# Two reorderings in a fused convolution and feed-forward kernel: the conversion of h in tile 21, and tile 1's first silu and up product

## What is computed

```python
def fake_quant(t, axis):
    s = jnp.max(jnp.abs(t), axis=axis, keepdims=True) / QMAX
    s = jnp.maximum(s, 1e-08)
    q = jnp.clip(jnp.round(t / s), -QMAX - 1.0, QMAX) * s
    return t + jax.lax.stop_gradient(q - t)
def qlinear(x, w):
    return jnp.einsum('bsh,oh->bso', fake_quant(x, axis=-1), fake_quant(w, axis=1))
out = lax.conv_general_dilated(x, weight, window_strides=(STRIDE,), padding=[(PAD, PAD)],
                               dimension_numbers=('NCH', 'OIH', 'NCH'), feature_group_count=GROUPS)
y = out + ctx[:, :, None] + bias[None, :, None]
gate = qlinear(y, w_gate)      # 512 -> 1376
up = qlinear(y, w_up)
h = jax.nn.silu(gate) * up
x + qlinear(h, w_down)         # 1376 -> 512
```

## Time and profile before

| what | us |
|---|---|
| median of 3 runs | 294.35 |
| lowest and highest run | 294.17 and 295.05 |
| the profiled execution | 294.47 |
| its span, first to last instruction | 292.9 |

### The profile page before, as it was taken

How to read it: one execution, slowest core, us unless ns; L and a number is a source line. 1 busy time by engine, 2 the same in 40 slices (tenths; PEclk the granted TensorE clock), 3 DMA queues, 4 the chain that set the end, 5 groups by cost and what they waited for, 6 DMA issues and landing times.

```text
span 292.9 us, 4778 instructions
## 1 busy us (share of the span) xinstructions
PE 281.7 (96%) x1621; PEld 164.4 (56%) x1621; DVE 251.0 (86%) x405; ACT 194.3 (66%) x232; POOL 202.0 (69%) x213
## 2 busy tenths in 40 slices
PE   7998999999999999999999999999989999999995
PEld 7897656655455555554444556665434444444443
DVE  3879879999998988989888878897978889888885
ACT  2258999996686666564888845455688866666640
POOL 1595899998776766663788835556578887666623
PEclk9999999999999999999999999999999999999999
DMA  7999963579846877755489996524256684433355
GB/s 261 416 408 357 410 133 72 113 166 273 214 144 160 203 168 165 208 149 119 128 214 299 239 241 195 166 49 124 73 157 157 159 177 114 87 86 85 100 99 202
DMA packets 83847, 53.36 MB, mean 182 GB/s; under 512 B 69904, under 2 KB 70672, under 8 KB 83696
## 3 DMA queue, kind: packets, MB, share of 16 engines
q1 hardware_dynamic: 83536, 52.89, 67.3%
q10 hardware_dynamic: 288, 0.18, 0.3%
HBM read 27.75 MB, written 8.39 MB: 123 GB/s over the span
## 4 chain that ended last, share of the span: by engine, by line
PE 64%; DVE 9%; POOL 9%; DMA 7%; ACT 5%; issue 4%; SPq 1%; DVEq 0%; POOLq 0%
PE bank L1047 38%; PE bank L1067 19%; PE bank L931 7%; POOL sg_mem L525 4%; DMA xq_mem<-yq_mem 3%; DMA slab<-x_windows 3%; DVE h_mem L813 2%; DVE h_max L819 2%; POOL xq_mem L499 1%; DVE y_part L745 1%; DMA hq_mem<-hq_mem 1%; DVE sg_mem L803 1%; DVE gu_max L704 1%; POOL y_mem L499 1%; ACT sg_mem L635 1%
## 5 line engine op out<-in xcount | busy, mean ns | idle before, releaser
L1047 PE MATMUL bank<-wgu_t,xq_mem 128*128 128x512 bf16 (+1 forms) x768 | 155.9, 357 | 3.1 <-DVE h_mem L813 2.0
L525 POOL TENSOR_TENSOR sg_mem<-sg_mem,gu_scale_row 128x512 f32<-128x512 f32 (+1 forms) x96 | 111.4, 1163 | 64.3 <-ACT sg_mem L635 64.0
L1047 PEld LDWEIGHTS bank<-wgu_t,xq_mem 128*128 128x128 bf16 x768 | 73.7, 98 | 75.2 <-DVE h_mem L813 8.8
L635 ACT ACTIVATE sg_mem<-sg_mem,x_scale 128x512 f32<-128x512 f32 (+1 forms) x96 | 63.7, 674 | 42.5 <-DVE sg_mem L803 42.1
L1067 PE MATMUL bank<-wd_t,hq_mem 128*128 128x512 bf16 (+1 forms) x341 | 78.6, 379 | 0.5 <-DMA hq_mem<-hq_mem 0.5
L813 DVE SCALAR_TENSOR_TENSOR h_mem<-bank,x_scale,sg_mem 128x512 f32<-128x512 f32 (+1 forms) x96 | 66.2, 691 | 10.3 <-POOL sg_mem L525 9.1
L803 DVE TENSOR_TENSOR sg_mem<-bank,gu_scale_row 128x512 f32<-128x512 f32 (+1 forms) x96 | 60.3, 628 | 16.0 <-PE bank L1047 15.6
L640 ACT ACTIVATE h_mem<-h_mem,h_inv 128x1376 f32<-128x1376 f32 (+1 forms) x32 | 45.3, 1414 | 28.1 <-DVE h_inv L697 28.0
L1067 PEld LDWEIGHTS bank<-wd_t,hq_mem 128*128 128x128 bf16 (+1 forms) x341 | 33.3, 98 | 40.9 <-DMA hq_mem<-hq_mem 1.0
L819 DVE TENSOR_REDUCE h_max<-h_mem 128x1 f32<-128x1376 f32 x32 | 50.4, 1576 | 0.0
L931 PE MATMUL bank<-toeplitz_cut,slab 128*128 128x160 f32 (+1 forms) x320 | 44.6, 290 | 1.9 <-DMA slab<-x_windows 1.7
(11 more groups left out here) (63 smaller groups left out, 138.4 us busy)
## 6 DMA issues: line engine op xcount, KB each, us to landing
slab<-x_windows SPq DMA_DIRECT2D x32, 320.0 KB, 5.4
xo_mem<-x SPq DMA_DIRECT2D x24, 256.0 KB, 3.0
out<-xo_mem SPq DMA_DIRECT2D x24, 256.0 KB, 2.2
hq_mem<-w_gate_up SPq DMA_DIRECT2D x6, 512.0 KB, 6.8
slab<-w_down SPq DMA_DIRECT2D x3, 688.0 KB, 12.5
h_mem<-w_gate_up SPq DMA_DIRECT2D x4, 512.0 KB, 13.6
slab<-x SPq DMA_DIRECT2D x1, 2048.0 KB, 9.3
out<-slab SPq DMA_DIRECT2D x7, 256.0 KB, 2.0
```

Source lines behind the costliest of these rows:

```text
L525: pool.tensor_tensor(s, s, gu_scale_row[:, 1, at:at + n], ALU.mult).then_inc(silu_scaled, 1)
L635: act.activation(s, s, ACT.Silu, scale=x_scale[:, i:i + 1]).then_inc(silu_done, 1)
L1047: last = pe.matmul(bank[n % 2][:, 0:cols], xq_t[:, g, k, P * c:P * (c + 1)], wgu_t[:, m, k, at:at + cols], start=(k == 0), stop=(k == KT - 1))
```

## The change

On ACT, in tile 21, `convert_h(20)` is issued ahead of `round_y(24)` and `round_y(25)` instead of behind them. In tile 0, ACT issues `silu(1, 0)` ahead of the rounding of channels 2 and 3 instead of behind it and the copy of a span, and POOL issues `scale_silu(1, 0)` ahead of the conversion of these channels. DVE issues `multiply_up(1, 0)` ahead of `token_scales(0)`. PE and SP have the same lists as before. No instruction is added or taken away.

```diff
@@ constants @@
-        FOLDS_AT[21] = [SLOTS - 1]
+        GROUP_3_AT = 21
+        FOLDS_AT[GROUP_3_AT] = [SLOTS - 1]
@@ gpsimd @@
             for i in range(TILES):
-                scale_silu(i, 0)
+                if i != 1:
+                    scale_silu(i, 0)
@@
                 scale_silu(i, 2)
+                if i == 0:
+                    scale_silu(1, 0)
                 for n in CHANNELS_AT.get(i, []):
                     convert_y(n)
@@ scalar @@
             for i in range(TILES):
+                if i > 1:
+                    silu(i, 0)
                 if i:
-                    silu(i, 0)
                     silu(i, 1)
@@
                 if i < TILES - 1:
                     silu(i, 2)
+                if i == 0:
+                    silu(1, 0)
+                if i == GROUP_3_AT:
+                    convert_h(i - 1)
                 for n in CHANNELS_AT.get(i, []):
                     round_y(n)
@@
-                if i:
+                if i and i != GROUP_3_AT:
                     convert_h(i - 1)
@@ vector @@
+                if i == 1:
+                    multiply_up(i, 0)
                 if i:
                     token_scales(i - 1)
@@
-                multiply_up(i, 0)
+                if i != 1:
+                    multiply_up(i, 0)
```

## The result

| | time, us |
|---|---|
| before, median of 20 (quickest to slowest) | 293.77 (293.69 to 295.05) |
| after, median of 20 (quickest to slowest) | 295.19 (293.73 to 296.44) |
| ratio after / before, 95% interval | 1.0037 [1.0027, 1.0048] |
| profiled execution of after, its span | 293.81, 292.2 |
| forecast | 293.47 (292.9 to 294.2) |

What follows compares the result with a forecast made beforehand. PE was taken as the bound from 75.7 to 131 and 215 to 270 us, with PE, ACT, DVE and POOL all busy from 49.1 to 63. Terms -1.23 and +0.35 on 294.35 gave 293.47 us, range 292.9 to 294.2.

Steps and rivals of the forecast that it cites:

- Term 1: Tile 21: h's conversion fits ACT's 2.06 us hole, so tile 22's product and up(22, 2) come earlier, -1.23 us.
- its last part: The prediction's closing list of what the changed profile would show if each part of the forecast is right or wrong.
- the 213.2 that was named as the sign against this term: Tile 22: a product starting later than 213.2 would show the forecast gain of -1.23 us wrong.
- Part 2's first half: Tile 1: the early silu and scaling start the product at 42.01, so up(1, 2) no longer waits for it.
- I take a value near the lower end, 2.5: Tile 2: channel 2's transpose, issued at 42.49, lands after 2.5 us at 45.0, against 45.06 for gate(2, 0) before.
- term 2: Tiles 1 to 6: PE gains nothing in tile 1 and delay on other engines reaches it, +0.35 us (0 to +0.75).
- the two ways that led to that term: Delay reaches PE through channel 6's transpose, 0.35 us later, or through up(2, 2) waiting for a product 0.24 to 0.31 later.
- Slower, by the transpose of channel 6: Rival: shifted by 0.35 us, channel 6's transpose may need 10.0 us, PE waits 2.27 more, 295.7 us; chance 0.08.
- Absorbed: Rival: the 0.35 us delay from tile 1 is absorbed by idle time on the engines, 293.1 us; chance 0.14.
- part 2 works: Rival: in tile 1 PE keeps its 0.93 us, needing channel 2 landed by 44.0, 292.2 us; chance 0.05.

Runs made afterwards that it cites:

- Part 1 alone: The kernel before with only the conversion of h in tile 21 moved and tiles 0 and 1 untouched: median 292.98 us, ratio 0.9966.
- the change with 16 empties: The full change with 16 instead of 22 empty matmuls at PE's start: median 292.86 us, 0.9961 of before.
- the change with no move on DVE: The full change, but multiply_up(1, 0) stays behind tile 0's row maximum on DVE: median 292.84 us, 0.9964 of before.
- part 1 with 36 empties: The kernel before with only tile 21's conversion of h moved, and 36 instead of 22 empty matmuls at PE's start: median 293.74 us, 0.9968 of before.

## Why the prediction was wrong

**Term 1, -1.23 us: right.** 1.21 us measured; the conversion in the hole, no wait of POOL ahead of `scale_silu(22, 0)`, and PE's idle time before up(22, 2) gone, as its last part asks for. The product of tile 22 starts at 213.60, beyond the 213.2 that was named as the sign against this term; but everything there comes 0.67 us later through tile 2, and without that it is 212.93, against 212.92 in the working. Part 1 alone moved the median by 292.98 - 293.91 = -0.93 and the quickest by -1.2 us.

**Part 2's first half: right.** The product was forecast at 42.01 and stands at 41.93, DVE's idle time before it at 0.24 and is 0.17; `round_h(0)` was forecast at 44.66 (44.59), channel 2's issue at 42.49 (42.43). The listed wait for L813 in tile 1 is gone, and a wait for xq_mem stands one group later, as its last part asks for, though of 2.25 us and not of about 1.

**The step that failed: "I take a value near the lower end, 2.5".** The landing took 3.8 us, and PE's wait was 2.25 us, not 1. I gave 3.3 as the bad end because before had it; and I saw only the queue ahead, not what else uses the DMA engines. The ground given, that the down weights' transpose is gone by then, was nearly right (it lands 0.9 us after channel 2's issue, and behind one like it channel 2 took 2.3); what was missing is the fetch packet that falls into the transpose. With 2.3, in the change with 16 empties, PE is 0.33 us late at tile 5, against a term 2 of +0.35. Of the two ways that led to that term one came: up(2, 2) waits for the later product. The other, by channel 6, did not: there channel 6 was issued at 68.37, some 0.4 us later with the start-up taken out, but landed after 7.05 us, not 7.73, and PE no longer waited for it; that both ways had given about the same number is luck. With 3.8 the term is +1.21. The whole gain of part 1 is eaten by this: 1.21 against 1.21.

**What was missing as well: the granted clock.** No rival had it. I moved a wait of 0.93 us from one group to the next and took it to be neutral; joined with the later landing it became one idle stretch of 2.25 us, after which half of the executions lost some 1.7 to 2 us more; by their mean clock of 0.992 to 0.994 they ran some 3.5 to 4.7 us at 1.2 GHz (an estimate: 0.6 to 0.8% of 292 us, times two). It gives the change its sign: the ten executions of after that kept the clock have a median of 294.04, 0.1% above before's.

**The rivals.** "Slower, by the transpose of channel 6" had the sign and, by luck, nearly the time, 295.7, but the wrong transfer: channel 6 cost nothing, since PE's wait for it was gone; it was channel 2. "Absorbed" and "part 2 works" did not come.

A version that beats both kernels is part 1 alone: 0.9966 [0.9951, 0.9981] of before. The whole change with 16 empties (0.9961) and the change with no move on DVE (0.9964) can't be told from it.

## What to carry to other kernels

Work put ahead of the step that issues a transfer is paid for by whoever waits for that transfer: cost the landing with the long values of its line as well as the short ones, and look at which other DMA queues have a packet there, since making an engine quicker moves its instruction fetches too. Before merging two short waits of TensorE into one long one, ask what the granted clock does after it, and compare the spread of executions and their mean clock, not the profiled execution alone. A part that gains where its engine had a hole (part 1) is best timed by itself.

## What the runs showed of the hardware

- One 16 KB instruction packet took 0.9 to 1.7 us here, and a transpose of 128x512 bf16 whose packets it fell among landed after 3.8 to 4.5 us instead of 2.3 to 3.4; the down weights' after 5.4 to 5.6 instead of 3.8 to 4.7. A channel's transpose queued close behind the down weights' landed 0.5 to 0.6 us after it: after 3.3 us in before, with no such packet near, and after 4.1 in part 1 with 36 empties, where the packet had delayed the down weights.
- Of the kernel whose profiled executions have 2.25 us of PE idle time, 15 of 30 executions have a mean granted clock of 0.992 to 0.994, and of one with 2.33 us, 4 of 4; the trace of the latter shows the clock at half right behind the idle time. What decides between falling and not falling is open.
